# A sum of the two channel tiles in place of x's first tile: attention and a circulant channel filter on one core

## The reference

```python
theta = einsum('bchw,kc->bkhw', x, theta_w)             # 32 rows
phi   = pool2(einsum('bchw,kc->bkhw', x, phi_w))        # 32 rows, 256 pooled pixels
beta  = softmax(theta^T phi)                            # 1024 x 256 per image
g     = pool2(einsum('bchw,kc->bkhw', x, g_w))          # 128 rows
o     = einsum('bchw,kc->bkhw', g beta^T, o_w)
x     = gamma * o + x
out   = x + einsum('fc,bchw->bfhw', toeplitz_circular(filter of 27 taps), x)
```

## Time and profile before

| what | value |
|---|---|
| median of 3 runs | 272.98 us (272.94 to 273.1) |
| span of the profiled execution, first to last instruction | 271.3 us |
| what lies around it (median less span) | 1.7 us |
| PE busy | 265.4 us, 98% |
| DVE busy | 245.9 us, 91% |
| ACT busy | 243.2 us, 90% |
| POOL busy | 149.6 us, 55% |
| granted TensorE clock, mean | 0.998 |

### The profile page before, as it was taken

One profiled execution on the slowest core, in us unless ns is written; L12 is line 12 of the kernel. 1 busy time (PEld: TensorE's weight loads), 2 busy tenths in 40 slices (PEclk: granted clock), 3 DMA queues, 4 the chain that ended last, 5 costly groups with the idle time before them and its releaser, 6 DMA issues.

```text
span 271.3 us, 4464 instructions
## 1 busy us (share of the span) xinstructions
PE 265.4 (98%) x1196; PEld 211.8 (78%) x1196; DVE 245.9 (91%) x456; ACT 243.2 (90%) x533; POOL 149.6 (55%) x79
## 2 busy tenths in 40 slices
PE   7999999999999999999999999999999999999994
PEld 3576778888888888888888888888887888888873
DVE  4998999999999999999999999999999999999953
ACT  4999999999999999998999999999999989998772
POOL 1585747574565747546673764667466475745100
PEclk9999999999999999999999999999999999999999
DMA  7978085582847657284673828467283855317044
GB/s 198 270 208 212 23 234 169 175 223 81 193 142 225 180 170 182 88 218 149 203 201 144 180 79 246 157 197 206 98 182 124 234 169 172 77 71 178 1 157 155
DMA packets 17380, 44.57 MB, mean 164 GB/s; under 512 B 2654, under 2 KB 3578, under 8 KB 16122
## 3 DMA queue, kind: packets, MB, share of 16 engines
q1 hardware_dynamic: 16682, 44.00, 56.4%
q10 hardware_dynamic: 688, 0.46, 0.5%
HBM read 17.45 MB, written 16.78 MB: 126 GB/s over the span
## 4 chain that ended last, share of the span: by engine, by line
PE 94%; DVE 2%; DMA 2%; ACT 0%; issue 0%; SPq 0%
PE psY L1009 10%; PE psY L988 8%; PE psY L990 7%; PE psY L989 7%; PE psV L1128 6%; PE psY L1112 6%; PE psY L1128 5%; PE psV L1112 5%; PE psV L988 3%; PE psV L990 3%; PE psV L989 3%; PE psX L1066 3%; PE psV L1096 3%; PE psV L1133 3%; PE psZ L1066 3%; PE psY L1118 3%
## 5 line engine op out<-in xcount | busy, mean ns | idle before, releaser
L457 POOL TENSOR_TENSOR prob_lo<-prob,prob_hi 128x1024 fp32r<-128x1024 f32 x30 | 72.1, 2404 | 59.7 <-ACT prob L537 32.5
L450 POOL TENSOR_TENSOR x_lo<-x_raw,x_hi 128x1024 fp32r<-128x1024 f32 x30 | 72.0, 2399 | 35.5 <-ACT x_hi L504 34.0
L504 ACT CAST x_hi<-x_raw 128x1024 fp32r<-128x1024 f32 x30 | 31.5, 1052 | 6.8 <-PE psY L1096 5.2
L526 ACT ACTIVATE psX<-psX,neg_max 128x256 f32<-128x256 f32 x60 | 26.7, 445 | 3.0 <-DVE neg_max L777 3.0
L526 ACT ACTIVATE psZ<-psZ,neg_max 128x256 f32<-128x256 f32 x60 | 27.4, 468 | 0.0
L709 DVE TENSOR_TENSOR thetaphi<-psY,thetaphi_rest 64x512 f32<-64x512 f32 x30 | 20.5, 682 | 3.8 <-ACT thetaphi_rest L508 3.1
L988 PE MATMUL psY<-x_hi,g_hi_w 128*128 128x512 f32 x56 | 22.2, 396 | 0.0
L990 PE MATMUL psY<-x_hi,g_lo_w 128*128 128x512 f32 x56 | 22.0, 393 | 0.0
L989 PE MATMUL psY<-x_lo,g_hi_w 128*128 128x512 f32 x56 | 22.0, 392 | 0.0
L715 DVE TENSOR_TENSOR theta_aug<-thetaphi,theta_aug 32x512 fp32r<-32x512 f32 x30 | 20.5, 683 | 0.9
L702 DVE TENSOR_REDUCE phi_pool<-thetaphi 32x128 f32<-32x512 f32 x30 | 20.2, 674 | 1.0
(11 more groups left out here) (189 smaller groups left out, 766.1 us busy)
## 6 DMA issues: line engine op xcount, KB each, us to landing
x_raw<-x SPq DMA_DIRECT2D x30, 512.0 KB, 5.1
out<-y SPq DMA_DIRECT2D x15, 1024.0 KB, 4.0
x_edge<-x_hi SPq DMA_DIRECT2D x64, 104.0 KB
x_edge<-x_lo SPq DMA_DIRECT2D x32, 104.0 KB
x_raw<-x SPq DMA_DIRECT2D x4, 256.0 KB, 4.5
out<-y SPq DMA_DIRECT2D x3, 256.0 KB, 2.1
band_rev<-ring SPq DMA_DIRECT2D x2, 128.0 KB, 6.9
out<-y ACTq DMA_DIRECT2D x1, 256.0 KB, 2.6
```

The source lines that it names most:

```text
L450: nc.gpsimd.tensor_tensor(x_lo[:, par, :, cols], x_raw[:, par, :, cols], x_hi[:, par, :, cols].bitcast(F32), ALU.subtract).then_inc(x_lo_r ...
L457: nc.gpsimd.tensor_tensor(prob_lo[:, h], prob[:, h], prob_hi[:, h].bitcast(F32), ALU.subtract).then_inc(prob_lo_ready, 1)
L504: nc.scalar.copy(x_hi[:, par, :, cols], x_raw[:, par, :, cols]).then_inc(x_hi_ready[h], 1)
L526: last = nc.scalar.activation(tiles[:, t, :], tiles[:, t, :], ACT.Exp, bias=neg_max[:, col:col + 1], accum_out=exp_sum[:, col:col + 1])
```

## The change

The first tile of x_raw is replaced, in place, by u = x0 + x1 (POOL, `add_tiles`), for the images 2 to 15; images 0 and 1 stay as they were (`is_raw`). Then PE accumulates in the banks of tile 0 the sum out0 + out1 = (D + E) u, which needs no corner product, and in those of tile 1 out1 = (D - E) x1 + E u, with one. DVE subtracts afterwards: out0 = sum - out1 (`rest_of_sum`). The projections' weights for x1 become differences, since W0 x0 + W1 x1 = W0 u + (W1 - W0) x1, and w2 for tile 0 a sum; these are made once in the prologue, by POOL. Theta's second high copy is no longer a cast on ACT but a transfer of 32 rows on SP's queue (`theta_copy`), behind the edge transfers, which now take one tile. With that the copies out of PSUM change hands: ACT copies tile 1 of both halves, DVE has the subtraction for tile 0 of both. The loop has one pair fewer, and one pair more is written out.

```diff
         def over_images(engine, image):
...
-            with engine.Fori(1, PAIRS - 1) as i:
+            with engine.Fori(1, PAIRS - 2) as i:
...
 # SP
+            def theta_copy(i, par, h):
+                cols = slice(h * HALF, (h + 1) * HALF)
+                sp.wait_ge(theta_hi_ready, upto(2, i, par, h + 1))
+                sp.dma_start(theta_aug[K:2 * K, par, cols].bitcast(F32),
+                             theta_aug[0:K, par, cols].bitcast(F32)).then_inc(theta_landed[h], 16)
...
                 if has_next(i, par):
                     x_edges(*following(i, par))
+                    for h in range(2):
+                        theta_copy(*following(i, par), h)
 # POOL
+            def add_tiles(i, par, h):
+                cols = slice(h * HALF, (h + 1) * HALF)
+                pool.wait_ge(x_loaded[h][par], 16 * (i + par))
+                nc.gpsimd.tensor_tensor(x_raw[:, par, 0, cols], x_raw[:, par, 0, cols], x_raw[:, par, 1, cols], ALU.add).then_inc(u_ready[h], 1)
...
-                if has_next_but_one(i, par):
-                    for h in range(2):
+                for h in range(2):
+                    if has_next_but_one(i, par):
                         x_low(i + 1, par, h)
...
+                    if has_next_but_two(i, par):
+                        ni, npar = following(i, par)
+                        add_tiles(ni + 1, npar, h)
 # ACT
-                for h in range(2):
-                    theta_copy(ni, npar, h)
                 if has_next_but_one(i, par):
                     x_high(i + 1, par, 0)
                 o_in_high(i, par, 0)
-                for h in range(2):
-                    exp_sums(ni, npar, h)
+                exp_sums(ni, npar, 0)
+                out_of_psum(i, par, 0, 1)
+                exp_sums(ni, npar, 1)
                 ln_sums(ni, npar)
                 if has_next_but_one(i, par):
                     x_high(i + 1, par, 1)
-                for f in (1, 0):
-                    out_of_psum(i, par, 1, f)
+                out_of_psum(i, par, 1, 1)
 # DVE
+            def rest_of_sum(i, par, h):
+                cols = slice(h * HALF, (h + 1) * HALF)
+                dve.wait_ge(out_evacuated[h][1], upto(1, i, par, 1))
+                dve.wait_ge(out_done[h][0], upto(1, i, par, 1))
+                dve.wait_ge(y_stored[par], 16 * i)
+                nc.vector.tensor_tensor(y[:, par, 0, cols], out_bank(i, par, h, 0), y[:, par, 1, cols],
+                                        ALU.subtract).then_inc(out_evacuated[h][0], 1)
...
                 maxima(ni, npar, 1)
-                out_of_psum(i, par, 0, 1)
                 o_in_high(i, par, 1)
-                out_of_psum(i, par, 0, 0)
+                if is_raw(i):
+                    out_of_psum(i, par, 0, 0)
+                else:
+                    rest_of_sum(i, par, 0)
                 o_in_low(i, par, 1)
                 shifts(ni, npar)
                 turn_shifts(ni, npar)
-                for h in range(2):
-                    spread_shifts(ni, npar, h)
+                spread_shifts(ni, npar, 0)
+                if is_raw(i):
+                    out_of_psum(i, par, 1, 0)
+                else:
+                    rest_of_sum(i, par, 1)
+                spread_shifts(ni, npar, 1)
 # PE
+                if f == 0 and not is_raw(i):
+                    last.then_inc(x_used[h], 1)
+                    return
                 other = 1 - f
                 last = nc.tensor.matmul(out_bank(i, par, h, f), edge_w[:, other * P:(other + 1) * P],
```

More of the change, by code:

```diff
@@ L241, in over_images @@
             image(0, 1)
-            with engine.Fori(1, PAIRS - 1) as i:
+            with engine.Fori(1, PAIRS - 2) as i:
                 image(i, 0)
                 image(i, 1)
-            image(PAIRS - 1, 0)
-            image(PAIRS - 1, 1)
+            for i in (PAIRS - 2, PAIRS - 1):
+                image(i, 0)
+                image(i, 1)
         def is_number(i):
@@ L255, in has_next_but_one, with has_next_but_two, is_raw @@
             return not (is_number(i) and i == PAIRS - 1)
+        def has_next_but_two(i, par):
+            return not is_number(i) or 2 * i + par + 3 < B
+        def is_raw(i):
+            return is_number(i) and i == 0
         def is_last(i, par):
@@ L955, in image @@
                     for h in range(2):
-                        out_of_psum(i, par, h, 0)
+                        rest_of_sum(i, par, h)
                     return
@@ L1003, in theta_phi @@
                     pe.wait_ge(thetaphi_summed, from_second(2, i, par, 1))
+                if is_number(i) and (i, par, h) == (1, 0, 0):
+                    pe.wait_ge(proj_dw_ready, 2)
+                weights = [tp_w[:, 0], tp_w[:, 1] if is_raw(i) else tp_dw[:]]
                 cols = slice(h * HALF, (h + 1) * HALF)
@@ L1022, in g_projection @@
                 for t in range(CT):
-                    last = three(g_bank(i, par, h), (g_hi_w[:, t, :], g_lo_w[:, t, :]), x_parts(par, t, h), t == 0, t == CT - 1)
+                    weights = (g_hi_w[:, t, :], g_lo_w[:, t, :]) if t == 0 or is_raw(i) else (g_hi_dw[:], g_lo_dw[:])
+                    last = three(g_bank(i, par, h), weights, x_parts(par, t, h), t == 0, t == CT - 1)
                 last.then_inc(g_done, 1)
@@ L1266, in image @@
                     for h in range(2):
-                        for f in range(CT):
+                        for f in (1, 0):
                             add_high_attention(i, par, h, f)
-                        for f in range(CT):
+                        for f in (1, 0):
                             add_low_attention(i, par, h, f)
```

121 lines of the change are left out of this document (102 added, 19 removed).

## The result

The changed kernel takes **304.31 us** (median of 4, 303.43 to 304.61) where the kernel before takes 273.03 (median of 4, run beside it): ratio 1.1141, 95% interval 1.1123 to 1.1159. I had forecast 286.0, range 277 to 293. The sign was right, the size was not. The profiled execution has a span of 301.7 us.

The account below looks back on a forecast made before the run. TensorE was taken to bound the kernel before, at 16.05 us an image, and the DVE and ACT round the changed one. First round at 34.41 plus 14 x 16.91, with the end, gave span 284.3, median 286.0; range 277 to 293.

Parts of the forecast that it names:

- S: Start on DVE of the sum of theta and phi, half 0, in each round; the first was taken at 34.41.
- I take S + 4: On SP: the six edge issues, starting at about S, end between S + 2.8 and S + 5.1; S + 4 taken.
- Theta lands late: Rival on SP: edge issues keep 0.84 each, theta lands S + 6.8 to S + 7.6; 293 us, at most 299; chance 0.14.
- the signs of being wrong: Period 15.6 with DVE idle ahead of S, scores waiting for a DMA, or granted clock under 1.00 from PE's gaps.
- up to 0.3 us, once: Prologue: of POOL's new operations only the add in front of x_high(1, 0, 1) shows, up to 0.3 us, once.
- the port rule: A DVE instruction with two SBUF inputs and a GpSimd instruction reading SBUF exclude each other, the later blocking fully.
- S to maxima: Stretch of the round on DVE from S to the next maxima: 7.42 us, bounds 7.31 and 7.53.
- the end: After the last round: 0.5 us more for DVE's subtraction behind ACT's copy, 0.2 less for one product fewer.
- The new round: Closed round of DVE and ACT with both insertions: 16.91 us, bounds 16.49 and 17.09, above PE's 15.59.
- rows 5 and 6: Trace rows pricing the moved operations: ACT's copy between exponentials 0.55 us; DVE's subtraction between spreads 0.84, making 2.15 to S.
- PE stays the bound: Rival on the round: both insertions add less than about 0.4 us, so the kernel is faster, 267.1 us; chance 0.08.
- the add collides: Rival on POOL: second add 0.7 us late blocks theta_low(0), up to 1.2 us an image; 294 us; chance 0.03.

Follow-up runs that it names:

- rows16: The changed kernel with edge groups of 16 partitions in place of 13, the extra rows meeting zero weights: 290.64 us.
- theta_act: The changed kernel with theta's second high copy back as a cast on ACT and no theta transfer on SP: 287.52 us.
- w2_psum: The changed kernel with w2's low part in the prologue read from PSUM and one SBUF operand, as before the change: 301.67 us.
- pool_rest_w2: pool_rest with w2's low part read from PSUM, as in w2_psum: 271.58 us.
- neither: theta_act with half 0's tile 1 copy back on DVE and half 1's subtraction left out, so that output part stays the sum: 272.01 us.
- pool_rest: neither with the missing subtraction done by GpSimd in SBUF, one round later, behind the add of half 0: 272.86 us.

## Why the prediction was wrong in size

**The step that failed** is "Theta's half 0 then goes out and has landed at most 2.1 us later: S + 6.1 ... Cost nothing, with 0.6 to spare." Its start (edges begin at S) and its landing (2.0) held. The time of the six issues ahead of it did not: "I take S + 4" was a middle between 0.47 for issues of the corner weights, which come from memory, and 0.84 for the very transfers in question. The middle supposed that half the bytes might halve the cost. They measured 5.38 us for six (0.90 each, one of the first four taking up to 1.38), and theta went out at S + 5.60 and landed at S + 7.6, so the scores waited and the maxima came at S + 8.40 and not at S + 7.42. before, changed and rows16 together show that half the bytes do not lower the price of an issue, while more partitions do. The near row was the edge transfers' own, and it should have been taken whole.

**The rival held the mechanism.** "Theta lands late" had the place, the price (0.1 to 0.9 a round) and the deciding point (0.77 each), with a chance of 0.14; the measured 1.20 a round (first to last S: 235.55 less theta_act's 219.96, over 13) is above its bound, also without the 0.12 of it that are the one round at the lower clock. That the clock would fall behind the wait was in the signs of being wrong, and in no sum.

**The account of the span**, 301.7 measured and 284.3 forecast, 17.4 (the profiled execution is the fastest of the four; the median lies 0.9 further out):

- theta late over the 13 rounds from first to last S: +15.6 (changed less theta_act). Of these 1.5 are the lower clock in the second round (19.91, where w2_psum with the same wait has 18.39), 14.1 the lateness itself.
- first S later than forecast: 35.98 - 34.41 = +1.6. I had "up to 0.3 us, once" for the prologue and looked only at the add; w2_low's two SBUF inputs were not weighed, though the port rule stood in my text. They are only a part: with w2_psum's edit the first S comes 0.32 earlier, in pool_rest_w2 0.85. The rest stays open.
- the first round's S to maxima, 8.80 for 7.42: +1.4, the casts under the add. The 13 rounds' own terms, -1.25: copy 0.46 for 0.55, and 7.31 to 7.46 for 7.42. Together theta_act's 219.96 against 13 x 16.91 = 219.83: +0.1.
- the last round, 271.53 to the end of the last spread at 288.40 + 0.68 = 289.08: 17.55 for 16.91, +0.6, late theta again.
- the end: -0.5.

**What was right.** The new round is set by the hand-offs of DVE and ACT and not by TensorE: theta_act has it at 16.92 where the sum was 16.91, and 287.52 where 286.0 was forecast. That the two agree to 0.01 is luck: in the loop the rounds are 16.74 and 16.90, below the sum because the copy took 0.46 (under my bound of 0.48), and the first round, 18.23, makes up for it. The two moved operations have about the prices that rows 5 and 6 gave them (0.50 for 0.55, 0.75 for 0.84). The rival "PE stays the bound" is what neither is: 15.70 in the loop, for 15.59 forecast.

**The rival "the add collides"** did not show in the loop of the changed kernel: theta_low(0) keeps 0.68 there. It showed once, on the casts of the second image, in w2_psum's prologue on theta_low, and in pool_rest's loop, where theta_low(0) takes up to 0.92.

## What to carry to other kernels

A transfer that replaces an engine's copy gets a place in a queue, and its price is the issue time of all that stands ahead of it: add those up from their own rows, at full price, and compare the landing with the first user before calling it hidden. Where several engines are over 90% busy, moving an operation is judged by the closed round, not by who has less to do: the same subtraction cost 0.75 us a round between two spreads on DVE, 0.06 in a gap of GpSimd, and 0.75 in another gap of GpSimd (16.56 against 15.81). Before an operand moves from PSUM to SBUF, look at what GpSimd does at that time.

## What the hardware showed that I had not expected

- The issue time of a transfer from SBUF to SBUF on the sync queue did not follow the bytes: 746 ns (median) for 13 partitions with 52 KB as with 104 KB, 592 for 16 partitions, 558 for 32.
- The same theta transfer of 64 KB landed in 2.0 us behind edge transfers of 52 KB, and in 3.3 to 3.4 behind those of 104 KB.
- A wait of 2.41 us of TensorE was followed by 4.95 us at a mean granted clock of 0.66, which made it cost 3.9 instead of 2.4. This came in twelve of 14 rounds; waits of 2.71 and 2.46 us in the other two left the clock at 1.00. In the changed kernel waits of 1.1 to 1.3 us left it at 1.00, and one of 1.60 us was followed by 3.40 us at 0.52, which cost 1.5 us, where one of 1.62 us in w2_psum was not. What else decides, no run here shows.
- VectorE's casts of 32 x 256 from SBUF to SBUF, two in 0.9 to 1.0 us in the loop, took 1.93 and 2.07 under GpSimd operations; a 128 x 256 subtraction took 2.25 with both inputs in SBUF and 0.47 with one in PSUM, both under GpSimd's subtraction.
